# Two orders of work on TensorE, in both layers of a two-layer model: projections around the router product, and transposes ahead of the intra products

## The chip, the core and the metric

The kernel runs on one core of a Trainium2 chip. The metric is the device time of one execution in microseconds. Its engines are TensorE (matrix products and transposes, with its weight loads), VectorE, ScalarE, GpSimd, and SyncE, which here only issues transfers. Each runs its own list of instructions in order and waits on semaphores that the others raise.

## The reference, cut to what matters

Two layers over 2 sequences of 2048 tokens of 256 numbers. Each layer normalizes its input and adds two branches to it.

```
x = L0_attn_x;  xn = layernorm(x)
x = x + mamba_block(xn) + soft_tree(xn)          # layer 0
xn = layernorm(x)
x = x + mamba2(xn) + expert_choice_moe(xn)       # layer 1

# layer 0's first branch
h = rmsnorm(xn);  v = xn + mamba2(h)             # 8 heads of 64, state 16, conv of 3 taps
mamba_block = v + silu(rmsnorm(v) @ mlp_w1 + b1) @ mlp_w2 + b2

# mamba2, for both layers
z, xBC, dt = split(h @ W_in);  dt = softplus(dt + dt_bias)
x, B, C = split(silu(causal_conv(xBC)))
state_t = state_{t-1} * exp(dt_t * A) + dt_t * x_t (outer) B_t
y_t = state_t . C_t + D * x_t
return rmsnorm(y * silu(z)) @ W_out              # layer 1: 4 heads of 128, state 64, 4 taps

# soft_tree: gate = sigmoid(xn @ Wq @ routers.T) over 255 nodes, leaf probabilities as
# products along 8 levels, @ leaf_values @ Wout
# moe: softmax(xn @ Wr), each of 8 experts takes its 1024 best tokens, gelu MLP, scatter-add
```

## The kernel before, in words

**Layer 0** goes over the tokens in 8 steps of 512, each of four chunks (tiles) of 128 tokens. A step has a front (mamba2 and the gates of the tree, for step f) and a back (tree output, MLP, next norm and router, for step b = f - 1). Both are in one loop body, written out by hand for each engine: `step0(f, b, n)` for TensorE stands at L2224, for ScalarE at L1113, for VectorE at L1614, where its arguments are (n, f, b). n = f + 1 is the step whose start is done at the end of the body. Steps 2 to 6 run in a hardware loop, the others are written out.

The order on TensorE around the change, at the end of a body: down products of the MLP; turned rows of n (hT); dt product of n; `in_proj(n, 0)`, which gives the B and C columns; the transposes of the next-layer rows (nT); the router product on nT (L2295). Then, in the next body, where n has become f: `decay_log_sums` (L2110: three products of 32 columns and one transpose, which wait for VectorE's softplus chain), `in_proj(f, 1)` to `in_proj(f, 4)` (the four blocks x0 to x3 of x), the transposes of the MLP's normed input (`turned(b, "h2T", ...)`), the gate products, and four of the eight up-products of the MLP (`up`, L2196). An up-product needs h2T in a high and a low half: ScalarE copies the high half h2Th (L1126), VectorE subtracts it for the low half h2Tl (L1629).

PSUM is used in four banks for these: two for the front, two for the back, each pair in turns. `open_front` and `open_back` let TensorE write a bank only when its last content has been read (for a projection: by both copies that ScalarE makes in `raw`, L1026; for an up-product: by the SiLU in ScalarE's `up`, L1107).

ScalarE's order at the same place: for n, turned rows, the exponential for dt, `raw(n, 0)`; the two nT copies; the exponential of the router's softmax; then in the next body `decay_exp`, `raw` of 1 to 4, the two h2T copies, the SiLUs of the convolutions and the tanh of the gates, and the SiLUs of the up-products among them. VectorE's order, which the diff leaves alone: dt and softplus, the copies of the router product and the softmax, the scores; then `normed` (xo, L1622), convolutions 0 to 3, `h2T_low`, convolution 4, the scans and chunks.

**Layer 1** (its mamba2) goes over 32 tiles of 128 tokens, four in a step, 8 steps, all written out (L2408 to L2433). For tile n TensorE does: `chunk1(n + 1)` (z, the turned x block xt, the small products, in steps 0 to 4 also a count product for the search of the experts' thresholds); `recur1(n)` (the product with the state, "inter"; the new state; the intra products E times Xdt); `y_turned1(n - 1)`, transposes of the gated y; in the first two tiles of a step two projections of the next step; `project1(n - 1)`, which waits for ScalarE's copy yT of the turned rows. In the third tile of a step the fifth projection comes ahead of `chunk1`. xt of tile n + 2 shares a bank with the state product of tile n, which VectorE reads in its state update (L1937). VectorE's sum of y (L1927) waits for the intra products; GpSimd then gates y (L938), makes the rms factor of the tile before (L946), and VectorE mixes (L1948).

The experts of layer 1 come last, from about 1183 us on; the change does not touch them.

Of the kernel before, what the change touches and what calls it, by code (L numbers as in the profile page):

```python
# [143 lines left out]
def program(nc, d, out):  # L144
    ctx = ExitStack()
    with ctx:
# [867 lines left out]
        def _(act):  # L1014
# [98 lines left out]
            def step0(f, b, n):  # L1113
# [14 lines left out]
                if f is not None:  # L1128
                    decay_exp(L, s, f)
                    for j in range(1, 5):  # L1130
                        raw(L, s, f, j)
                if b is not None:
                    h2T_copies()
                if f is not None:
                    conv_silu(L, s, f, 0)
                    conv_silu(L, s, f, 1)
                    gates(L, s, f)
                for j in EARLY_UPS:
                    if f is not None and j < 3:
                        conv_silu(L, s, f, j + 2)  # L1140
                    if b is not None:
                        up(b, j)
# [23 lines left out]
                if b is not None:  # L1166
                    for k in range(2):
                        p = back_wait(act, b, f"nT{k}")

                        back_wait(act, b - 1, "rt1")  # L1170
                        nT_stored.wait_ge(act, b, 0)
                        a.activation(nT[:, :, 2 * P * k:2 * P * (k + 1)],
                                     p[:, :].rearrange("p (k n) -> p k n", k=KD), ACT.Copy).then_inc(nT_sig.sem, 1)
                    smx_sig.wait_ge(act, b, 1)
                    a.activation(sx[:, 1, :, :], sx[:, 0, :, :], ACT.Exp).then_inc(sme_sig.sem, 1)
# [3 lines left out]
            raw(LAYERS[0], sets[0], 0, 0)  # L1179
            step0(0, None, 1)  # L1180
# [891 lines left out]
        def _(pe):  # L2072
# [151 lines left out]
            def step0(f, b, n):  # L2224
                L, s = LAYERS[0], sets[0]

                if f is not None:
                    decay_log_sums(L, s, f)
                    for j in range(1, 5):
                        in_proj(L, s, f, j)  # L2230
                if b is not None:
                    turned(b, "h2T", xo, h2_sig, CH)
                if f is not None:
                    gates(L, s, f)
# [41 lines left out]
                if b is not None:  # L2276
                    for g in range(2):
# [6 lines left out]
                        back_filled(last, f"nT{g}")  # L2284
                    for g in range(2):
# [10 lines left out]
            in_proj(LAYERS[0], sets[0], 0, 0)  # L2296
            step0(0, None, 1)
# [57 lines left out]
            def recur1(i, c):  # L2355
                q, cb, n = c % 2, CB[i % 2], CH * i + c
# [6 lines left out]
                filled1(mm(p[0:64, :], Bs[:, q, :], Xs[:, q, :]), "state")  # L2363
# [44 lines left out]
            for n in range(TILES1):  # L2408
# [7 lines left out]
                if n:  # L2416
                    y_turned1(*divmod(n - 1, CH))
                if following and c < 2:
# [145 lines left out]
```

## Time and profile before

| | us |
|---|---|
| median of 3 runs | 1607.27 |
| runs | 1602.73, 1607.27, 1607.95 |
| the profiled execution | 1599.53 |
| its span, from first to last instruction | 1597.7 |

The profile is of the one execution in the third line. Its page gives the busy time of each engine as a share of the span. In this kernel layer 0 fills about the first 785 us, the mamba part of layer 1 runs to about 1183 us, the experts to the end. PE is TensorE's matrix unit and PEld its weight loads, DVE is VectorE, ACT is ScalarE, POOL is GpSimd, SPq is SyncE's queue. A row of a timeline gives the start, the duration, the engine, the source line and the operation with its output and inputs, how many instructions it merges, and in brackets the idle time just before it with the instruction that ended it. Many products share the helper's line L2076; they are told apart by their operands: `hT,m0wbc` is projection 0 of layer 0, `hT,m0big` with 16 instructions are the projections x0 to x3 (two weight blocks, each in two instructions), `wr,nT` the router product, `h2Th,w1h` the first of an up-product's six, `EW,hT` the gates.

### The profile page before, as it was taken

Reading aid. Unit: us, or ns where it says so; the run is one execution under the profiler, and the core shown is the slowest. Engines: PE = TensorE matmul, PEld = TensorE weight load, DVE = VectorE, ACT = ScalarE, POOL = GpSimd, SP = SyncE. Lnnn points to the kernel's source line nnn. Section 1 sums busy time; section 2 is a strip of 40 time slices with the busy share of each in tenths; the row PEclk is TensorE's granted clock in tenths of the full one; section 3 lists DMA queues with packets and bytes.
Section 4 is the critical chain, followed back from the end, with each engine's and each line's share of the span. In section 5 each row is a group of like instructions: output and inputs, shape, how many; then the busy total and the mean of one; then the engine's idle time right before and its main releaser. Section 6 shows DMA issues by size and latency. Waiting matters only on the chain.

```text
span 1597.7 us, 22669 instructions
## 1 busy us (share of the span) xinstructions
PE 1462.5 (92%) x7315; PEld 1062.9 (67%) x7315; DVE 1082.6 (68%) x2557; ACT 725.6 (45%) x1468; POOL 534.0 (33%) x631
## 2 busy tenths in 40 slices
PE   4879999999999999997788888999889999999996
PEld 2546767677676867676544555555459888898895
DVE  4878677686867676762588888878865555546542
ACT  1434252524334252522165556555455555555552
POOL 1242424142433424231112233233343434544343
PEclk8999999999999999997799999999999999999998
DMA  6110030302021120201221111212023334343332
GB/s 212 53 54 27 20 100 1 106 13 93 26 82 37 39 80 0 94 14 40 95 93 37 66 63 37 66 63 67 27 62 99 61 87 106 77 97 62 87 54 27
DMA packets 71846, 100.90 MB, mean 63 GB/s; under 512 B 13000, under 2 KB 58192, under 8 KB 71760
## 3 DMA queue, kind: packets, MB, share of 16 engines
q1 hardware_dynamic: 59472, 82.77, 15.9%
q0 software_dynamic: 12288, 17.05, 6.4%
q8 instruction: 46, 0.75, 0.2%
q14 instruction: 40, 0.33, 0.1%
HBM read 74.30 MB, written 25.49 MB: 62 GB/s over the span
## 4 chain that ended last, share of the span: by engine, by line
PE 63%; issue 15%; DVE 8%; POOL 7%; ACT 4%; DMA 1%; SPq 1%; PEldq 0%; POOLq 0%; ACTq 0%; DVEq 0%; PEld 0%
PE bank L2076 59%; POOL yb L938 2%; POOL Xs L930 2%; POOL ry L946 1%; PE bank L2186 1%; PE bank L2443 1%; PE bank L2154 1%; DVE am L1890 1%; POOL out L994 1%; DVE dts L1497 1%; PE bank L2212 1%; ACT am L1111 1%; ACT tg L1072 1%; POOL ry L943 1%; ACT u L1049 0%
## 5 line engine op out<-in xcount | busy, mean ns | idle before, releaser
L2031 DVE TENSOR_TENSOR aml<-m0big,amh 128x512 fp32r<-128x512 f32 x128 | 88.2, 689 | 162.8 <-ACT amh L1327 153.3
L994 POOL DMA_INDIRECT out<-EW,IDX x64 | 105.1, 1643 | 223.7 <-DVE EW L2016 209.0
L1322 ACT ACTIVATE m0big<-bank,eb 128x512 f32<-128x512 f32 x128 | 88.0, 687 | 147.6 <-PE bank L2076 125.6
L2076 PE MATMUL bank<-w2h,amh 128*128 128x256 f32 x512 | 147.9, 289 | 0.0
L2076 PE MATMUL bank<-w2h,aml 128*128 128x256 f32 x512 | 144.8, 283 | 0.0
L2076 PE MATMUL bank<-w2l,amh 128*128 128x256 f32 x512 | 144.7, 283 | 0.0
L2076 PE MATMUL bank<-EW,am 128*128 128x256 f32 x512 | 115.8, 379 | 0.0
L1111 ACT ACTIVATE am<-bank,b 128x512 f32<-128x512 f32 x64 | 43.7, 683 | 150.0 <-PE bank L2076 149.4
L2076 PEld LDWEIGHTS bank<-EW,am 128*128 128x128 f32 x512 | 97.2, 190 | 13.5 <-ACT am L1111 0.3
L2076 PE MATMUL bank<-xTh,w1h 128*128 128x512 f32 x256 | 102.3, 399 | 2.8 <-DVE w1l L2022 2.8
L2076 PEld LDWEIGHTS bank<-w2h,amh 128*128 128x128 f32 x512 | 97.6, 191 | 8.3 <-issue 5.8
L2076 PE MATMUL bank<-xTl,w1h 128*128 128x512 f32 x256 | 100.6, 393 | 0.0
L2076 PE MATMUL bank<-xTh,w1l 128*128 128x512 f32 x256 | 99.6, 389 | 0.0
L2076 PEld LDWEIGHTS bank<-w2l,amh 128*128 128x128 f32 x512 | 97.8, 191 | 2.2
L938 POOL TENSOR_TENSOR yb<-yb,zs 128x512 f32<-128x512 f32 x32 | 40.6, 1269 | 171.8 <-DVE yb L1927 171.8
L2076 PEld LDWEIGHTS bank<-w2h,aml 128*128 128x128 f32 x512 | 97.7, 191 | 0.0
L2076 PEld LDWEIGHTS bank<-Xdt,E 128*128 128x128 f32 x512 | 64.3, 201 | 42.9 <-issue 38.9
L1327 ACT ACTIVATE amh<-m0big 128x512 fp32r<-128x512 f32 x128 | 80.9, 632 | 4.0
L2076 PE MATMUL bank<-Xs,Bs 128*64 128x512 f32 x128 | 72.3, 648 | 11.3 <-POOL Xs L930 6.6
L834 POOL TENSOR_TENSOR xb<-x,xp 128x256 f32<-128x256 f32 x32 | 22.4, 728 | 172.3 <-ACT u L1049 164.3
L2076 PE MATMUL bank<-EW,yT 128*128 128x256 f32 x256 | 62.5, 387 | 13.1 <-ACT yT L1248 12.4
L969 POOL DMA_INDIRECT xg<-rows_d,IDX x64 | 67.1, 1048 | 19.3 <-issue 19.0
(336 smaller groups left out, 3695.9 us busy)
## 6 DMA issues: line engine op xcount, KB each, us to landing
EW<-in_e_w SPq DMA_DIRECT2D x16, 1024.0 KB, 5.9
dA0b<-dA_d SPq DMA_DIRECT2D x16, 512.0 KB, 3.8
E<-dA_d SPq DMA_DIRECT2D x16, 512.0 KB, 5.4
m0big<-dA_d SPq DMA_DIRECT2D x16, 512.0 KB, 4.7
xin<-in_L_attn_x SPq DMA_DIRECT2D x8, 512.0 KB
xp<-in_L_attn_x SPq DMA_DIRECT2D x8, 512.0 KB, 3.9
rows_d<-xo SPq DMA_DIRECT2D x8, 512.0 KB, 3.0
x_d<-xb SPq DMA_DIRECT2D x8, 512.0 KB, 4.1
```

The costliest lines, as they stand in the source:

```text
L834: g.tensor_tensor(xb[:, c, :], x2[:, c, :], xp[:, c, :], ALU.add).then_inc(xb_sig.sem, 1)
L930: g.tensor_tensor(Xs[:, q, :].rearrange("p (h e) -> p h e", h=NH1), x3, WEND[:, hd].unsqueeze(2).to_broadcast([P, NH1, P]), ALU.mult).then ...
L938: g.tensor_tensor(yb[:, q, :], yb[:, q, :], zs[:, q, :], ALU.mult).then_inc(s1.yg.sem, 1)
L943: g.tensor_scalar(ry[:, c:c + 1], ssq[:, c:c + 1], 1.0 / DI, 1e-5, ALU.mult, ALU.add).then_inc(s1.rv.sem, 1)
L946: g.tensor_tensor(ry[:, c:c + 1], ry[:, c:c + 1], nhalf[:, 0:1], ALU.pow).then_inc(s1.ry.sem, 1)
L969: g.indirect_dma_start(out=xg[:, q, c, :], out_offset=None, in_=rows_d, in_offset=bass.IndirectOffsetOnAxis(ap=IDX[:, 4 * u + c:4 * u + c ...
L994: g.indirect_dma_start(out=out_rows, out_offset=bass.IndirectOffsetOnAxis(ap=IDX[:, 4 * u + c:4 * u + c + 1], axis=0), in_=ye[:, q, c, :], ...
L1111: a.activation(am[:, k, :], p[:, :], ACT.Silu, bias=b1[:, k:k + 1]).then_inc(am_sig.sem, 1)
L1322: a.activation(am2[:, j % 2, :], bank[j % 2][:, :], ACT.Gelu, bias=eb1[:, u // 2, j:j + 1]).then_inc(gelu_sig.sem, 1)
L1327: a.activation(amh[:, j % 4, :], am2[:, j % 2, :], ACT.Copy).then_inc(am_high.sem, 1)
L2031: v.tensor_tensor(aml[:, j % 4, :], am2[:, j % 2, :], amh[:, j % 4, :], ALU.subtract).then_inc(am_low.sem, 1)
L2076: return t.matmul(out_, lhsT, rhs, start=first, stop=last)
```

## The change

In layer 0 the projection x0 of the next step moves from the start of the next body to the end of this one, between the nT transposes and the router product. The start of a body becomes: x1, decay sums, x2, h2T transposes, x3, gates. ScalarE's copies move in the same way: `raw(n, 1)` behind the nT copies and ahead of the router's exponential; then `raw` 2, `decay_exp`, `raw` 3, h2T copies, `raw` 4. Each of ScalarE's early up-SiLUs goes ahead of the convolution's SiLU that stood before it. For the first step, x0 is done ahead of the first body. In layer 1 `recur1` is cut in two, and the transposes `y_turned1(n - 1)` go between the state product and the intra products.

```diff
@@ ScalarE, step0
                 if f is not None:
+                    raw(L, s, f, 2)
                     decay_exp(L, s, f)
-                    for j in range(1, 5):
-                        raw(L, s, f, j)
+                    raw(L, s, f, 3)
                 if b is not None:
                     h2T_copies()
                 if f is not None:
+                    raw(L, s, f, 4)
                     conv_silu(L, s, f, 0)
                     conv_silu(L, s, f, 1)
                     gates(L, s, f)
                 for j in EARLY_UPS:
+                    if b is not None:
+                        up(b, j)
                     if f is not None and j < 3:
                         conv_silu(L, s, f, j + 2)
-                    if b is not None:
-                        up(b, j)
...
+                if n is not None:
+                    raw(L, s, n, 1)
+                if b is not None:
                     smx_sig.wait_ge(act, b, 1)
                     a.activation(sx[:, 1, :, :], sx[:, 0, :, :], ACT.Exp).then_inc(sme_sig.sem, 1)
...
             raw(LAYERS[0], sets[0], 0, 0)
+            raw(LAYERS[0], sets[0], 0, 1)
             step0(0, None, 1)
@@ TensorE, step0
                 if f is not None:
+                    in_proj(L, s, f, 2)
                     decay_log_sums(L, s, f)
-                    for j in range(1, 5):
-                        in_proj(L, s, f, j)
+                    in_proj(L, s, f, 3)
                 if b is not None:
                     turned(b, "h2T", xo, h2_sig, CH)
                 if f is not None:
+                    in_proj(L, s, f, 4)
                     gates(L, s, f)
...
                         back_filled(last, f"nT{g}")
+                if n is not None:
+                    in_proj(L, s, n, 1)
+                if b is not None:
                     for g in range(2):
                         p = open_back(pe, b, f"rt{g}")
...
             in_proj(LAYERS[0], sets[0], 0, 0)
+            in_proj(LAYERS[0], sets[0], 0, 1)
             step0(0, None, 1)
@@ TensorE, layer 1
                 p = open1("state", n)
-                filled1(mm(p[0:64, :], Bs[:, q, :], Xs[:, q, :]), "state")
+                filled1(mm(p[0:64, :], Bs[:, c % 2, :], Xs[:, c % 2, :]), "state")
+
+            def intra1(i, c):
+                q = c % 2
                 s1.y0.wait_ge(pe, i, c)
                 s1.xdt.wait_ge(pe, i, c + 1)
                 s1.M.wait_ge(pe, i, c + 1)
...
                 recur1(i, c)
                 if n:
                     y_turned1(*divmod(n - 1, CH))
+                intra1(i, c)
```

## Rows read from the trace of the kernel before

**Rows 1.** The page: busy time and share of each engine; one DMA issue.

```profile
PE 1462.5 (92%) x7315; PEld 1062.9 (67%) x7315; DVE 1082.6 (68%) x2557; ACT 725.6 (45%) x1468; POOL 534.0 (33%) x631
...
dA0b<-dA_d SPq DMA_DIRECT2D x16, 512.0 KB, 3.8
```

**Rows 2.** Timeline of TensorE, boundary into step 4: start, duration, instruction, idle before.

```profile
373.53 1.96 PE L2076 MATMUL bank<-hT,m0wbc 128*128 128x512 f32 x4
375.33 1.04 PE L2282 MATMUL bank<-ident,xo 128*128 128x128 f32 x8
377.43 1.93 PE L2076 MATMUL bank<-wr,nT 128*128 128x12 f32 x16 [1.06 <-ACT nT L1172]
...
380.35 8.73 PE L2076 MATMUL bank<-hT,m0big 128*128 128x512 f32 x16
...
389.79 3.62 PE L2076 MATMUL bank<-EW,hT 128*128 128x256 f32 x16
393.06 0.58 PE L2076 MATMUL bank<-h2Th,w1h 128*128 128x512 f32 x1
...
397.05 0.50 PE L2076 MATMUL bank<-h2Th,w1h 128*128 128x512 f32 x1 [0.86 <-ACT am L1111]
```

**Rows 3.** Windows: busy time of PE, PEld, DVE, ACT, POOL; PEclk; DMA share; GB/s.

```profile
382.00:384.00 2.00, 2.00 (x3) 0.78 (x3) 1.97 (x6) 0.27 (x1) 0.00 (x0) 0.50 0.64 55
...
1000.00:1002.00 2.00, 2.00 (x7) 1.29 (x7) 1.96 (x6) 0.34 (x2) 0.00 (x0) 0.54 0.95 356
```

**Rows 4.** Timeline of ScalarE, the same boundary.

```profile
376.68 1.08 ACT L1172 ACTIVATE nT<-bank 128x512 f32<-128x512 f32 x2
...
390.27 1.08 ACT L1126 ACTIVATE h2Th<-bank 128x512 fp32r<-128x512 f32 x2
```

**Rows 5.** Timeline of VectorE, the same boundary and the first chunk behind it.

```profile
379.33 0.27 DVE L1708 COPY rtb<-bank 128x24 f32<-128x24 f32 x2
...
382.86 1.53 DVE L1461 SCALAR_TENSOR_TENSOR u<-xbuf,m0conv,u 128x512 f32<-128x512 f32 x2
...
385.03 1.54 DVE L1461 SCALAR_TENSOR_TENSOR u<-xbuf,m0conv,u 128x512 f32<-128x512 f32 x2 [0.25 <-ACT xbuf L1039]
...
390.90 1.29 DVE L1629 TENSOR_TENSOR h2Tl<-bank,h2Th 128x512 fp32r<-128x512 f32 x2 [0.40 <-ACT h2Th L1126]
...
404.24 0.17 DVE L1555 COPY Bs<-bank 128x16 f32<-128x16 f32 x1 [7.60 <-PE bank L2162]
```

**Rows 6.** Timeline of SyncE's queue, the same boundary: the first load of decay rows.

```profile
386.05 0.34 SPq L665 DMA_DIRECT2D dA0b<-dA_d  x1
```

**Rows 7.** Timeline of TensorE at the boundaries into steps 0, 1 and 2.

```profile
53.67 1.98 PE L2076 MATMUL bank<-m0big,hT 128*128 128x512 f32 x4 [1.73 <-ACT tg L1072]
...
108.73 0.64 PE L2076 MATMUL bank<-dtv,triU 128*128 128x32 f32 x2 [5.01 <-DVE dtv L1509]
...
126.40 0.47 PE L2076 MATMUL bank<-h2Th,w1h 128*128 128x512 f32 x1 [2.75 <-DVE h2Tl L1629]
...
198.42 2.38 PE L2076 MATMUL bank<-wr,nT 128*128 128x12 f32 x16 [1.06 <-ACT nT L1172]
...
219.32 0.50 PE L2076 MATMUL bank<-h2Th,w1h 128*128 128x512 f32 x1 [0.86 <-ACT am L1111]
```

**Rows 8.** Timeline of VectorE at the boundary into step 1.

```profile
115.18 1.54 DVE L1461 SCALAR_TENSOR_TENSOR u<-xbuf,m0conv,u 128x512 f32<-128x512 f32 x2 [3.75 <-ACT xbuf L1039]
```

**Rows 9.** Waits of TensorE, 780 to 1200 us: total us, times, longest us.

```profile
PE bank L2076 <- ACT yT L1248: 12.4, 18, 0.7
```

**Rows 10.** Timeline of TensorE in layer 1, step 3, behind a third and a fourth tile.

```profile
996.32 0.63 PE L2345 MATMUL bank<-ident,u 128*128 128x128 f32 x4 [2.51 <-DVE S L1937]
...
1003.52 1.99 PE L2076 MATMUL bank<-EW,yT 128*128 128x256 f32 x8 [0.69 <-ACT yT L1248]
```

**Rows 11.** Timeline of VectorE in layer 1: in step 3, and in step 6's first tile.

```profile
1008.29 0.16 DVE L1805 TENSOR_SCALAR okm<-bank 128x3 int32<-128x3 f32 x1 [0.76 <-PE bank L2353]
...
1105.33 3.12 DVE L1890 SCALAR_TENSOR_TENSOR am<-xbuf,m1conv,am 128x512 f32<-128x512 f32 x4 [1.67 <-ACT xbuf L1204]
```

More of the change, by code:

```diff
@@ L2355, in recur1 @@
             def recur1(i, c):
-                q, cb, n = c % 2, CB[i % 2], CH * i + c
+                cb, n = CB[i % 2], CH * i + c
                 s1.bs.wait_ge(pe, i, c + 1)
```

## The prediction

> **What bounds the kernel now.** I read the busy shares first: TensorE is the busiest engine by far [rows 1]. A busy TensorE is modelled, though, so the next view is its own order of work over one boundary between two steps of layer 0, with its idle time. There it stands idle 1.06 us for the next-layer rows nT, ahead of the router product, and 0.86 us ahead of the third up-product, until ScalarE has emptied the bank of the first [rows 2]. The same two waits stand in the boundary into step 2 and in the ones after it, six in all, within 0.1 us [rows 7]. Third, the granted clock: behind the short products (router, decay sums) TensorE drops to 1.2 GHz, level 0.50, for over 3 us [rows 3]. Its 16 projection instructions there take 8.73 us; by the four of the first projection, (1.96 - 0.24) / 4 = 0.43 each with a tail of 0.24, they would take 7.1, so this costs 1.6 us [rows 2]. From there to the next boundary TensorE has no wait over 0.4 us: layer 0 is TensorE-bound except in those places.
>
> In layer 1, TensorE's list of waits has 18 of 0.69 us for yT [rows 9]; between them it waits for VectorE's state update, 2.51 us in the place shown, one of six [rows 10]. There the two engines take turns as the bound.
>
> **Layer 0, a steady boundary** (the times are those of the boundary into step 4). The eight nT transposes end near 376.2 (0.9 us from 375.33). Today TensorE then waits until 377.43 [rows 2]. With projection x0 there (four instructions, 1.7 us) it reaches the router product at 377.9, when ScalarE's nT copies (376.68 to 377.76) are done [rows 4]. So the 1.06 wait is filled, and the router product comes 0.5 us later, ending at 379.8. Projection x1 covers the wait for the decays; then the sums (0.8), x2 (1.7), the h2T transposes (0.9), x3 (1.7), the gates (3.3): TensorE could start the up-products at about 390.0, against 393.06 now [rows 2]. Here I assume full clock: full-width projections now stand among the short products.
>
> But the up-products wait for the low half of h2T, which VectorE makes behind the normed rows and four convolutions, and the change leaves VectorE's order alone. Today it is done at 390.90 + 1.29 = 392.2 [rows 5], hidden under the gates. In the changed order the router's copy on VectorE, at 379.33 today, gets its second half only at about 379.8, so softmax, score rows and normed rows come 0.35 us later. The convolutions lose their waits, 0.25 before the second and 0.40 before h2Tl [rows 5], because x0 and x1 are ready early and h2Th, which ScalarE copies at 390.27 today [rows 4], is ready before 387. That makes 392.2 + 0.35 - 0.65 = 391.9, and the up-products start at 392.0 instead of 393.06: **1.05 us won**, with a new TensorE wait of 2 us in front of them. The clock's 1.6 us hide in that wait, so whether the low stretch goes changes little.
>
> The up-products themselves: ScalarE today does the last projection's copies, two h2Th copies, a table load, five SiLUs and four tanhs without rest, and so reads the first up-bank late. The third product starts at 397.05; six instructions at the pace of the others (0.23 each, twice) after 393.06, with 0.2 for the first, would let it start at 396.02. That is **1.03 us to win**: with h2Th copied before the last projection, and each up-bank read ahead of a convolution's SiLU, ScalarE is through with the tanhs at 392.6 and reads the first bank at 393.8, before the third product is due at 394.9. Bounds: 0.6 if ScalarE stays half behind, 1.2 if the start is smoother.
>
> Together 2.1 us. The lower bound is 1.0 (the ScalarE part alone), the upper 3.7 (1.06 + 1.6 + 1.03, all of TensorE's, were VectorE no limit). I take 2.1, by VectorE's own rows. Five such boundaries give 10.5. The boundary into step 2 has a longer low stretch: from the router product to the third up-product it takes 219.32 - 198.42 = 20.90 us against 19.62 later [rows 2, 7], so 1.3 more may go there: 3.4.
>
> What the moved work drags along: the decays' exponentials come 2.2 us later on ScalarE, behind x1's copies. On SyncE the first load of them is issued at 386.05 today [rows 6]; 2.2 later and with 3.8 to land [rows 1] they are there at 392.1. VectorE's first scan wants them at 393.5, and has 7.60 us of idle time behind it [rows 5]. The next-layer stores stand ahead of this on SyncE's queue and wait for nothing that comes later but the score rows, by 0.35. GpSimd's residual sum waits for the last SiLU, which comes earlier. All free; if that cover were gone, each us past it would count.
>
> **Layer 0, the first boundaries.** Into step 1, TensorE waits 5.01 us for the decays, then 2.75 for h2Tl, behind VectorE's preparation of weights [rows 7]. With x0 and x1 in the first wait, VectorE loses its 3.75 us wait before the second convolution [rows 8]. But TensorE then idles some 7 us before the up-products and starts them at 1.2 GHz, which takes 1.7 to 3.4 us back. I take 1.5. Into step 0 two projections come ahead of the sums; later TensorE stalls 1.73 us for the tanhs [rows 7], and this is what can be won: 1.7, between 0 and 2.5. **Layer 0: 10.5 + 3.4 + 1.5 + 1.7 = 17.1 us.**
>
> **Layer 1.** In the third and fourth tile of each step, and in all of the last, the order is intra products (1.0 us), y transposes (0.44), a copy on ScalarE (0.60), project, which waits 0.69 [rows 9, 10]. With the transposes first, the intra products cover the copy and project starts 0.85 earlier. What that is worth:
> - third tiles: TensorE then waits for VectorE's state anyway (2.51, [rows 10]). Nothing.
> - fourth tiles of steps 0 to 4: VectorE waits 0.76 us for TensorE's count product behind them [rows 11], so 0.76 each: 3.8.
> - step 5: both gains pass into VectorE's wait of 1.67 us for a projection [rows 11]: 1.5.
> - steps 6 and 7: VectorE and GpSimd mostly set the pace with the one-hot rows: 1.6, between 0 and 3.
> - The intra products end 0.44 later. VectorE asks for them later still in nearly all tiles. Free; 0.44 a tile (32 tiles: 14 us) if I misread this.
>
> Sum 6.9. Against it stands the clock: behind the 2.51 us wait TensorE fell to 1.2 GHz (granted 0.54 from 1000 to 1002) [rows 3]. That wait grows to 3.4, and I charge one further low stretch like that of layer 0: 1.7. **Layer 1: 5.2 us**, between -1 and 9.
>
> The Trainium skill, "TensorE: Matmul & The Clock Gate", Part 1 (The HAM clock gate) and the section on HAM oscillation, has TensorE throttled by default, released by activity, and cold again behind an idle gap; that speaks against both new waits. The trace agrees in layer 1, while in layer 0 the clock fell behind short products and a wait of only 1.06 us. [...]
>
> **The sum:** 17.1 + 5.2 = 22.3, say 22 us. The profiled execution took 1599.5 us (span 1597.7 and 1.8 around it); it would become 1577.5. It lies 8 us under the median of the runs shown, 1607.3, and below all three; on the median the forecast is 1607.3 - 22 = **1585 us**.
>
> **The rivals.**
> - *The router's delay eats VectorE's lead* (0.17): the copy chain behind the later router product costs as much as the saved waits. A boundary gives 1.0, layer 0 gives 5.0 + 2.3 + 3.2 = 10.5, in all 16: 1591. For it: that chain has hardly a gap. Against: the 0.65 us of waits are plain rows.
> - *TensorE alone sets layer 0* (0.08): no new wait before the up-products; 5 x 3.7 + 5.0 + 3.2 + 5.2 = 32: 1575. Against it: the four convolutions in a row.
> - *Layer 1 gives nothing* (0.12), all absorbed by VectorE: 1590.
> - *The change doesn't do what it says* (0.05): h2T is turned early but VectorE reaches it no sooner and ScalarE stays behind, and layer 1's transposes wait for GpSimd's gated rows in their new place. Some 3 us: 1604.
> - *Slower, by the clock* (0.05): the new 2 us wait puts the up-products at 1.2 GHz, and layer 1's longer waits do the same. Price: two low stretches a boundary, at the 1.7 each, are 6 x 3.4 = 20, and two more in each of five steps of layer 1 are 17; 37 against the 24 (17.1 + 6.9) won: 1620. It decides from 48 us of new low time, half of it lost. For it: layer 1's rows. Against: the wait stands between gates and up-products, both dense.
>
> **How the numbers follow.** The forecast has 0.53. The range from 1570 (a little under the second rival) to 1600 leaves out the last two rivals and the edges of the others, under 2 in 10. A measurement of this kernel can tell 0.3%, 4.8 us, from no change. Faster by more: the forecast and the first three rivals, less a little at their edge, 0.88. Within it: the fourth and that edge, 0.07. Slower: 0.05.
>
> **What the profile of the changed kernel would show.** At each steady boundary: no wait before the router product; a wait of 1 to 2 us for h2Tl before the first up-product; none for am before the third; steps 86.8 us apart instead of 88.9. In layer 1: the 0.69 us waits gone, the waits for the state some 0.8 longer. The prediction is wrong if the steps come 85 or 88 us apart, if the wait before the up-products carries another name than h2Tl, or if the granted clock is 0.50 inside the up-products.

## The result, and the profile after

| | before | after |
|---|---|---|
| median, us | 1607.0 | 1578.5 |
| runs, lowest to highest, us | 1602.7 to 1608.0 | 1576.5 to 1581.2 |
| the profiled execution, us | 1599.5 | 1576.5 |
| its span, us | 1597.7 | 1574.6 |

The ratio of after to before is 0.984, 95% interval 0.982 to 0.986: faster by 25.7 us of 1607, between 22.5 and 28.9. The forecast was 1585, 22 us. To see where the 23 us of the two profiled executions lie, I cut both traces at three places: the first product of each projection 0 in layer 0, the first of layer 1, and the first of the experts.

| stretch, us | before | after | won | forecast |
|---|---|---|---|---|
| to projection 0 of step 1 | 101.8 | 99.4 | 2.4 | 1.7 |
| to that of step 2 | 92.8 | 90.5 | 2.3 | 1.5 |
| to that of step 3 (boundary into step 2) | 90.15 | 85.7 | 4.45 | 3.4 |
| one steady step, to that of step 4, 5, 6 and 7 (four of them) | 88.9 | 86.3 | 2.6 | 2.1 |
| from projection 0 of step 7 to layer 1 | 148.5 | 144.0 | 4.5 | 2.1 |
| layer 0 | 788.6 | 764.7 | 23.9 | 17.1 |
| layer 1, mamba part | 398.4 | 398.3 | 0.1 | 5.2 |
| experts | 410.7 | 411.6 | -0.9 | 0 |

The page of after, busy time of each engine, against [rows 1]:

```profile
PE 1453.0 (92%) x7315; PEld 1061.9 (67%) x7315; DVE 1079.9 (69%) x2557; ACT 727.3 (46%) x1468; POOL 533.4 (34%) x631
```

TensorE does the same 7315 products in 9.5 us less busy time. By stretch, it is 15.9 us less in layer 0 (717.0 to 701.1), where the granted clock rose from 0.95 to 0.97, and 5.4 more in layer 1's mamba part, where it fell from 0.96 to 0.93. How much of the 9.5 us is the clock's wasn't taken apart. Its timeline at the boundary into step 4 answers to [rows 2]:

```profile
361.91 1.96 PE L2081 MATMUL bank<-hT,m0wbc 128*128 128x512 f32 x4
363.71 1.04 PE L2288 MATMUL bank<-ident,xo 128*128 128x128 f32 x8
364.58 1.88 PE L2081 MATMUL bank<-hT,m0big 128*128 128x512 f32 x4
366.31 1.85 PE L2081 MATMUL bank<-wr,nT 128*128 128x12 f32 x16
...
374.82 3.62 PE L2081 MATMUL bank<-EW,hT 128*128 128x256 f32 x16
380.05 0.50 PE L2081 MATMUL bank<-h2Th,w1h 128*128 128x512 f32 x1 [1.61 <-DVE h2Tl L1634]
...
386.66 0.66 PE L2217 MATMUL bank<-ident,leaf 128*128 128x128 f32 x4 [0.34 <-ACT am L1111]
```

The wait ahead of the router product is gone, and so is the one ahead of the third up-product; a wait of 1.61 us for h2Tl stands before the first. VectorE at the same place, against [rows 5]:

```profile
370.56 1.14 DVE L1627 TENSOR_SCALAR xo<-x,ry 128x256 f32<-128x256 f32 x4 [0.51 <-issue]
371.62 1.53 DVE L1466 SCALAR_TENSOR_TENSOR u<-xbuf,m0conv,u 128x512 f32<-128x512 f32 x2
...
376.86 1.53 DVE L1466 SCALAR_TENSOR_TENSOR u<-xbuf,m0conv,u 128x512 f32<-128x512 f32 x2
378.43 0.23 DVE L1477 TENSOR_SCALAR xbuf<-xbuf,flags 128x2 f32<-128x2 f32 x1
378.63 1.29 DVE L1634 TENSOR_TENSOR h2Tl<-bank,h2Th 128x512 fp32r<-128x512 f32 x2
```

Four convolutions in a row, then h2Tl without a wait: from 371.62 to h2Tl VectorE has no gap over 0.2 us. In layer 1, TensorE behind a third tile (step 3) and behind the next, against [rows 10], and the clock of the first of these stretches:

```profile
971.68 1.09 PE L2355 MATMUL bank<-ident,u 128*128 128x128 f32 x4 [3.44 <-DVE S L1942]
...
977.46 1.02 PE L2388 MATMUL bank<-ident,yb 128*128 128x128 f32 x4
978.31 1.05 PE L2081 MATMUL bank<-Xdt,E 128*128 128x128 f32 x8
979.20 1.95 PE L2081 MATMUL bank<-EW,yT 128*128 128x256 f32 x8
980.99 1.88 PE L2081 MATMUL bank<-EW,hT 128*128 128x512 f32 x4
982.71 0.60 PE L2355 MATMUL bank<-ident,u 128*128 128x128 f32 x4
```

```profile
971.60:975.00 3.40, 3.32 (x11) 2.39 (x11) 1.49 (x6) 2.23 (x6) 2.03 (x4) 0.50 0.18 48
975.00:978.40 3.40, 3.40 (x8) 1.23 (x8) 3.26 (x10) 1.75 (x6) 0.00 (x0) 0.52 0.82 295
978.40:981.80 3.40, 3.40 (x19) 2.77 (x18) 2.50 (x7) 0.60 (x1) 1.27 (x1) 1.00 0.01 4
```

The products of the transposed y start with no wait. But the wait for the state is 3.44 us instead of 2.51, and TensorE runs at 1.2 GHz (granted 0.50 and 0.52) for twice as long behind it, 6.8 us against 3.4. From the end of the wait to the next tile it needs 982.71 - 971.68 = 11.03 us; before it was 1007.07 - 996.32 = 10.75.

### The profile page after: what moved, and what is told of

Its sections match the earlier page's. It is cut to its first block, busy times and chain, and to the rows that moved or that the text cites. A ratio compares the mean times of both kernels' runs of the same rounds, so it can differ in the third digit from the quotient of the medians.

```text
span 1574.6 us, 22674 instructions
## 1 busy us (share of the span) xinstructions
PE 1453.0 (92%) x7315; PEld 1061.9 (67%) x7315; DVE 1079.9 (69%) x2557; ACT 727.3 (46%) x1468; POOL 533.4 (34%) x631
## 4 chain that ended last, share of the span: by engine, by line
PE 63%; issue 15%; DVE 10%; POOL 7%; ACT 2%; DMA 1%; SPq 0%; DVEq 0%; PEldq 0%; POOLq 0%; PEld 0%; ACTq 0%
PE bank L2081 59%; DVE u L1466 3%; POOL yb L938 2%; POOL Xs L930 2%; POOL ry L946 1%; PE bank L2191 1%; PE bank L2457 1%; PE bank L2159 1%; DVE am L1895 1%; POOL out L994 1%; DVE xo L1627 1%; PE bank L2288 1%; POOL ry L943 1%; PE bank L2135 0%; SPq L586 0%
## 5 line engine op out<-in xcount | busy, mean ns | idle before, releaser
L2081 PE MATMUL bank<-Xdt,E 128*128 128x64 f32 (+1 forms) x512 | 69.0, 285 | 0.0
```

The lines of the kernel that those rows point to most:

```text
L2081: return t.matmul(out_, lhsT, rhs, start=first, stop=last)
```

## The experiments

Each run is given with its ratio to the kernel before, 95% interval behind it, and the landmarks of its profiled execution ("layer 0" is the time at which layer 1's first projection starts, "layer 1" from there to the experts). "Step" is the distance of projections 0 in the steady part of layer 0. A "low stretch" is a time in which TensorE's granted clock is 0.50 (1.2 GHz).

**Each layer alone.** Layer 1 back in the old order:

```diff
-            def intra1(i, c):
-                q = c % 2
                 s1.y0.wait_ge(pe, i, c)
...
-                intra1(i, c)
```

> The changed kernel without its layer 1 part. In the changed kernel's trace layer 0 ends 23.9 us earlier than before (first product of layer 1 at 764.7 instead of 788.6), and the mamba part of layer 1 takes 398.3 instead of 398.4 us. Theory: all of the gain is layer 0's, so this kernel is as fast as the changed one: 23 to 28 us faster than before, ratio 0.984 +- 0.002, with layer 1 at 398 us and single low stretches of the clock. Rival (layer 1 wins 5 us when alone, and layer 0's new timing spoils it by chance of phase): this one loses 5 us against the changed kernel, ratio 0.988.

Measured: 0.9858 (0.9832 to 0.9884), 1584.9 us. Step 86.3, layer 0 770.5, layer 1 402.1, with low stretches of 10.2 us in two places instead of the single ones expected. The other half, layer 1's edit on the kernel before:

> The kernel before with the y transposes ahead of the intra products, alone. Theory: the 0.69 us waits for yT go, the wait for VectorE's state grows to 3.4 us and the stretch at 1.2 GHz behind it doubles, so that nothing is left: 0 to 1 us, ratio 1.000, layer 1 at 398 us. Forecast of the prediction: 5.2 us, ratio 0.997. If the low stretches stay single here, 4 us faster.

Measured: 0.9983 (0.9965 to 1.0001), 1601.1 us. Step 88.85, layer 0 788.8, layer 1 398.6, with low stretches of 6.8 us behind the waits for the state, as the theory had it.

So layer 0 carries 22.8 us (1.42% of 1606; 18.6 to 27) and layer 1 alone 2.7 us, hardly to be told from nothing. That the profiled executions give 18.1 and 23.9 us for the same code of layer 0 (with and without layer 1's edit) was a surprise that has its own paragraph below.

**Layer 0 taken apart.** First x0 of the next step ahead of the router product, with the last projection (x3) and each early up-SiLU left where they were, and layer 1 in the old order (the cut shows ScalarE, against the kernel after):

```diff
+                    raw(L, s, f, 4)
                 if b is not None:
                     h2T_copies()
                 if f is not None:
-                    raw(L, s, f, 4)
...
-                    if b is not None:
-                        up(b, j)
                     if f is not None and j < 3:
                         conv_silu(L, s, f, j + 2)
+                    if b is not None:
+                        up(b, j)
```

and in_proj(f, 4) ahead of the h2T transposes on TensorE.

> The kernel before with projection x0 of the next step ahead of the router product and x1 ahead of the decay sums, alone: h2T is turned behind all projections, and ScalarE's up-SiLUs keep their old places. Theory by the trace (what counts is x0 early: it fills the 1.06 us wait, feeds VectorE's convolutions and ScalarE's copies): the up-products start 1.4 us earlier, and the wait of the third up-product shrinks from 0.86 to 0.3 or less, as ScalarE ends its h2T copies 3 us earlier; steps 86.4 to 86.9 us apart against 88.9, 18 to 22 us in all, ratio 0.987. Rival (the turning of h2T is needed for the ScalarE part, 1.0 to 1.2 per boundary): steps 87.5 apart, 10 to 13 us, ratio 0.993.

Measured: 0.9846 (0.9818 to 0.9873), 1582.5 us. Step 86.26, layer 0 769.0: a little more than the theory had, and far from the rival's 87.5. Its boundary into step 4:

```profile
377.68 3.62 PE L2081 MATMUL bank<-EW,hT 128*128 128x256 f32 x16
382.92 0.50 PE L2081 MATMUL bank<-h2Th,w1h 128*128 128x512 f32 x1 [1.62 <-DVE h2Tl L1634]
```

From its projection 0 (364.78) to this first up-product it is 18.14 us, and in the kernel after 380.05 - 361.91 = 18.14 too. Then the other part by itself, h2T turned ahead of the last projection and up-SiLUs first, with x0 at its old place:

> The kernel before with h2T turned ahead of the last projection and ScalarE's early up-SiLUs ahead of the convolutions' SiLUs, alone; x0 stays behind the decay sums. Theory: the 1.06 us wait and the low clock stay, the up-products start where they did (the gates end there), and only the 0.86 us wait for am goes: steps 87.8 apart, 1.0 to 1.2 per boundary, 7 to 8 us in all, ratio 0.995. Rival (turning h2T early is the main part, since VectorE waited 0.40 us for it): 1.5 or more per boundary, 11 us, ratio 0.993.

Measured: 0.9951 (0.9932 to 0.997), 1597.5 us. Step 88.25 (87.8 expected), but 86.55 in one, that from 284.28 to 370.83. The boundary at the start of that step, and the next one, with the clock of each:

```profile
288.17 1.93 PE L2077 MATMUL bank<-wr,nT 128*128 128x12 f32 x16 [1.06 <-ACT nT L1173]
...
291.09 5.32 PE L2077 MATMUL bank<-hT,m0big 128*128 128x512 f32 x12
...
305.47 0.50 PE L2077 MATMUL bank<-h2Th,w1h 128*128 128x512 f32 x1 [0.24 <-ACT am L1111]
...
374.73 1.93 PE L2077 MATMUL bank<-wr,nT 128*128 128x12 f32 x16 [1.06 <-ACT nT L1173]
...
377.78 6.87 PE L2077 MATMUL bank<-hT,m0big 128*128 128x512 f32 x12
...
393.71 0.50 PE L2077 MATMUL bank<-h2Th,w1h 128*128 128x512 f32 x1 [0.24 <-ACT am L1111]
```

```profile
292.00:294.00 2.00, 2.00 (x6) 0.90 (x5) 1.44 (x6) 0.99 (x2) 0.00 (x0) 1.00 0.40 17
...
378.00:380.00 2.00, 2.00 (x3) 0.79 (x3) 1.29 (x7) 0.40 (x2) 0.00 (x0) 0.50 0.14 10
```

Both boundaries have the same waits; the one has its 12 projection instructions in 5.32 us, the other in 6.87. That is a clean price for a low stretch of 3.4 us on TensorE's path: 88.25 - 86.55 = 1.70 us. The reorder itself gives 88.86 - 88.25 = 0.6 a step, not the 1.0 to 1.2 expected, since the third up-product's wait shrinks from 0.86 to 0.24. On top of x0's move it gives nothing: both kernels have steps of 86.3.

To see whether the filled wait of 1.06 us was what counted, x0 of the next step also moved to the end of the body, but behind the router product, so that the wait stays:

```diff
-                if n is not None:
-                    in_proj(L, s, n, 1)
                 if b is not None:
                     for g in range(2):
                         p = open_back(pe, b, f"rt{g}")
...
+                if n is not None:
+                    in_proj(L, s, n, 1)
```

(ScalarE's `raw(n, 1)` likewise behind the router's exponential; the rest as in the run with x0 alone.)

> Layer 0 only: projection x0 of the next step at the end of the body, but behind the router product instead of ahead of it (and ScalarE's copies of it behind the router's exponential); the rest as in the run with x0 alone, whose steps are 86.3 us apart. The 1.06 us wait for nT comes back, and the router's copy on VectorE is no longer delayed by 0.38 us. Theory (VectorE's chain sets the boundary, so TensorE's wait is worth nothing by itself; feeding the convolutions early is what counts): steps 85.9 to 86.3 apart, if the clock stays up. Rival (filling the 1.06 us wait is the gain): steps 87.2 to 87.4 apart. If the clock falls here again for 3.4 us, up to 0.5 us on top in either case, as the wait for h2Tl hides most of it.

Measured: 0.9952 (0.9934 to 0.997), 1598.3 us. Step 88.51, and 86.77 in the one step (283.07 to 369.84) without a low stretch. A step with one, and the clock there:

```profile
373.74 1.99 PE L2080 MATMUL bank<-wr,nT 128*128 128x12 f32 x16 [1.06 <-ACT nT L1173]
...
392.99 0.50 PE L2080 MATMUL bank<-h2Th,w1h 128*128 128x512 f32 x1 [0.85 <-ACT am L1111]
```

```profile
377.00:379.00 2.00, 2.00 (x3) 0.67 (x2) 1.30 (x7) 0.00 (x0) 0.00 (x0) 0.53 0.14 10
```

This boundary has no wait for h2Tl: with the 1.06 us wait and the low stretch in place TensorE is itself late enough. It costs 88.51 - 86.26 = 2.25 us a step against x0 ahead of the router product, and 1.74 of it goes when the clock stays up. The other 0.51 is neither the theory's (85.9 to 86.3 at full clock) nor the rival's (87.2 to 87.4). The step without a low stretch shows where it lies:

```profile
283.07 1.96 PE L2080 MATMUL bank<-hT,m0wbc 128*128 128x512 f32 x4
...
286.97 1.93 PE L2080 MATMUL bank<-wr,nT 128*128 128x12 f32 x16 [1.06 <-ACT nT L1173]
...
300.87 0.49 PE L2080 MATMUL bank<-h2Th,w1h 128*128 128x512 f32 x1
...
304.52 0.50 PE L2080 MATMUL bank<-h2Th,w1h 128*128 128x512 f32 x1 [0.60 <-ACT am L1111]
```

From projection 0 to the first up-product it is 300.87 - 283.07 = 17.80 us here, although the wait for nT is still there; in the kernel after, without that wait, it is 18.14. The run with h2T turned early and x0 at its old place has 17.82 in its step without a low stretch (302.10 - 284.28). So at the first up-product the wait costs nothing by itself as long as VectorE is the limit; what it costs comes with the low stretch (19.16 us with one). The 0.51 lies behind it: from the first up-product to the second group of turned leaves it is 7.45 us here and 6.61 in the kernel after, 0.84 more, with a wait of 0.60 us for ScalarE ahead of the third up-product. Whether the low stretch goes because the wait is filled, or because a projection now stands between the transposes and the router product, no run separates. With the wait in place the low stretch was absent in one or two of the six boundaries of these two runs; with x0 ahead of the router product it was absent in all of them.

**VectorE as the new bound of the boundary.** On the kernel after, h2Tl is made one convolution earlier:

```diff
-                    for j in range(4):
+                    for j in range(3):
                         conv(L, s, f, j, dve0)
                         keep_halo(L, s, f, j)
...
                     h2T_low()
-                    conv(L, s, f, 4, dve0)
-                    keep_halo(L, s, f, 4)
+                    for j in range(3, 5):
+                        conv(L, s, f, j, dve0)
+                        keep_halo(L, s, f, j)
```

> The changed kernel with one move on VectorE: the low half of h2T (h2Tl) ahead of the fourth convolution instead of behind it. Theory: in the changed kernel VectorE's chain sets when the up-products start, TensorE waiting 1.6 us for h2Tl at each steady boundary; h2Th is there 2.2 us before VectorE takes it. So this wait goes: steps 84.7 us apart instead of 86.3, about 10 us in all, ratio 0.978 against before. Rival (TensorE's own products, or ScalarE's SiLUs behind the later fourth convolution, take over at once): steps 85.8 or more, under 3 us.

Measured: 0.9771 (0.9745 to 0.9797), 1567.2 us: 37 us under before by the ratio, and 11 under after. Step 84.90, layer 0 755.4. VectorE, and TensorE's up-products, at the same boundary:

```profile
370.57 1.53 DVE L1466 SCALAR_TENSOR_TENSOR u<-xbuf,m0conv,u 128x512 f32<-128x512 f32 x2
372.34 1.29 DVE L1634 TENSOR_TENSOR h2Tl<-bank,h2Th 128x512 fp32r<-128x512 f32 x2
```

```profile
370.23 3.62 PE L2082 MATMUL bank<-EW,hT 128*128 128x256 f32 x16
...
376.87 0.50 PE L2082 MATMUL bank<-h2Th,w1h 128*128 128x512 f32 x1
```

No row between those two of TensorE carries a wait. 88.86 - 84.90 = 3.96 us a boundary: this is what TensorE's own waits and low stretch were worth, the 3.7 of the prediction's second rival. The first up-product comes 373.76 - 357.33 = 16.43 us behind projection 0, where it was 19.53 before and 18.14 after: with VectorE out of the way the filled wait counts too.

**Layer 1: what took the gain.** To keep TensorE's clock up, the z product of a step's first tile (which waits for the state of the third tile before) is preceded by two repeats of itself; the real product overwrites them.

```diff
                 p = open1("z", n)
+                if c == 0 and i:
+                    for _ in range(2):
+                        for k in range(KD):
+                            mm(p[:, :], (hT, h2T)[i % 2][:, k, cols(c)], W[1]["z"][:, k, :], k == 0, k == 1)
```

On the kernel after:

> The changed kernel with filler work in layer 1: ahead of the first tile of each step but step 0, TensorE does the z products twice more (8 instructions, 3.4 us, same bank, their result written over), where it now waits 1.7 to 4.1 us for VectorE's state. Nothing else changes. Theory (the gain of the moved transposes in layer 1 is eaten by the clock, which falls to 1.2 GHz for 6.8 us behind this wait): the low stretches there go, and the mamba part of layer 1 takes 393 us instead of 398.3, 1.0 us less in each of six steps, until VectorE sets the pace. Rival (VectorE absorbs it, the clock costs nothing): 397.5 us or more.

Measured: 0.9833 (0.9808 to 0.9859), 1577.3 us. Layer 1 395.75, between the two readings. TensorE's waits for the state between 780 and 1180 us there, and in the kernel after without the repeats (total us, times, longest):

```profile
PE bank L2359 <- DVE S L1942: 5.5, 7, 0.9
```

```profile
PE bank L2355 <- DVE S L1942: 19.5, 7, 4.1
```

On the kernel before:

> The kernel before with the same filler in layer 1. Its waits there are 0.7 to 3.2 us, so up to 2.7 us of the filler stand on the path in step 5 and 1 us in the others. Theory (clock): the low stretches, 3.4 us each, go; layer 1 takes 394 to 397 instead of 398.4, and 1 to 3 us more than the changed kernel with filler, because each 0.69 us wait for yT in the fourth tiles is still there. Rival (VectorE sets the pace once the clock is held, whatever the order of the transposes): the same 393 as the changed kernel with filler.

Measured: 0.9981 (0.9964 to 0.9998), 1603.9 us. Layer 1 398.45, with no low stretch behind 819 us: over the 394 to 397 of the theory. The totals say little by themselves; the steps of layer 1 say more (us between projections 0, in brackets the length of the low stretch in it):

| step of layer 1 | before | after | before, repeats | after, repeats |
|---|---|---|---|---|
| 0 | 48.2 (6.8) | 47.1 (6.8) | 45.7 | 45.6 |
| 1 | 48.1 (3.4) | 48.2 (6.8) | 47.5 | 48.3 (3.4) |
| 2 | 47.9 (3.4) | 48.1 (6.8) | 47.5 | 48.2 (3.4) |
| 3 | 47.9 (3.4) | 48.1 (6.8) | 47.5 | 46.7 |
| 4 | 44.7 | 46.4 (6.8) | 47.2 | 45.2 |
| 5 | 45.5 | 44.1 | 48.9 | 46.9 |

In the new order the low stretches cost 1.2 to 1.5 us a step where the repeats removed them (steps 0, 3 and 4). In steps 1 and 2 one of 3.4 us is left, and nothing is won; in step 5, which had none, the repeats cost 2.9 us. In the old order the repeats won 2.4 us in step 0 and 0.4 to 0.6 in each of steps 1 to 3, so its low stretches cost something too. But in steps 4 and 5, where it waited 0.7 us or not at all, they stand on TensorE's path and cost 2.5 and 3.4. So 398.32 - 395.75 = 2.6 us and 398.45 - 395.75 = 2.7 us are sums of gains and losses. What the new order would be worth at full clock throughout, and so whether the 6.9 us that I had summed were right, these two runs leave open. The waits in the kernel before, in the same view:

```profile
PE bank L2345 <- DVE S L1937: 13.6, 6, 3.2
PE bank L2076 <- ACT yT L1248: 11.7, 17, 0.7
```

Of the 17 waits for yT one is left in the kernel after, 11.0 us less; the waits for the state took 19.5 - 13.6 = 5.9 of this back, and the lower clock about the rest. The windows over all of layer 1's mamba part have a granted clock of 0.96 before and 0.93 after:

```profile
788.60:1187.00 398.40, 350.26 (x1362) 200.41 (x1362) 336.43 (x816) 221.83 (x556) 119.22 (x136) 0.96 0.18 59
```

```profile
764.70:1163.00 398.30, 355.63 (x1362) 204.96 (x1362) 336.19 (x815) 223.96 (x556) 117.03 (x136) 0.93 0.18 60
```

The same 1362 products were 5.4 us longer busy.

**Making the state earlier.** The wait for the state is long in the third tile because VectorE does the fifth convolution of the next step ahead of it. On the kernel with h2Tl earlier:

```diff
-                if following and c == 2:
-                    conv1(i + 1, 4)
                 sums1(i, c)
+                if following and c == 2:
+                    conv1(i + 1, 4)
```

> The kernel with h2Tl ahead of convolution 3, and besides, in layer 1's third tile, VectorE makes the sum of y and the state before the fifth convolution of the next step instead of behind it. Theory 1 (the state wait is VectorE's order: the convolution, about 3.1 us, stands in front of the state): the state comes 3.1 us earlier, TensorE's waits of 3.4 us behind the third tiles fall under 0.5, the convolution fills VectorE's 1.31 us wait for GpSimd's rms factor, and layer 1 goes from 398.5 to 386 to 392 us. Theory 2 (VectorE's total of work sets layer 1 and its waits only move): under 3 us, the waits for the state turn up in the fourth tile instead, layer 1 at 396 to 399.

Measured: 0.9833 (0.98 to 0.9866), 1576.3 us. Layer 1 405.65: 7 us longer, a miss of both theories. TensorE, ScalarE and VectorE in the place where the wait for the state was:

```profile
965.81 1.11 PE L2356 MATMUL bank<-ident,u 128*128 128x128 f32 x4 [4.02 <-ACT u L1219]
```

```profile
965.13 0.63 ACT L1219 ACTIVATE u<-u 128x512 f32<-128x512 f32 x1 [6.07 <-DVE u L1896]
```

```profile
962.59 2.51 DVE L1896 SCALAR_TENSOR_TENSOR u<-xbuf,m1conv,u 128x512 f32<-128x512 f32 x3
...
968.01 0.16 DVE L1811 TENSOR_SCALAR okm<-bank 128x3 int32<-128x3 f32 x1 [2.22 <-PE bank L2364]
```

TensorE needs both results of VectorE there, the state and, through ScalarE's SiLU u, the fifth convolution. The two take VectorE 5.3 us in either order, so whichever comes second ends at the same time, and the convolution has the SiLU of 0.63 us behind it: the wait went from 3.44 to 4.02 us. Step 0 and steps 2 to 4 are 0.4 to 0.7 us longer, about this growth. The rest of the 7 us lies in step 1 (50.1 against 48.2 us, with a low stretch of 10.2 us instead of 6.8) and in step 5 (46.6 against 44.1, with a new wait of 1.48 us for u and a low stretch of 3.4 behind it). The convolution does fill VectorE's wait for GpSimd, but the wait for TensorE behind it (okm) grew from 0.53 to 2.22. The bracket of a wait names the last releaser alone; the one behind it was some 2 us away. The same edit with layer 1 in the old order, and h2Tl earlier with layer 1 in the old order:

> Both: the state ahead of the fifth convolution, layer 1's transposes in the old order. If the new order was worth nothing only because the state's wait behind it took its gain back, then with the state early it is worth 2 to 7 us: this one is that much slower in layer 1 than the one with the new order. If it is worth nothing for another reason, both take the same within 1.5 us.

> The kernel with h2Tl ahead of convolution 3, with layer 1 in the old order (y's transposes behind the intra products). If the new order of layer 1 is worth nothing while the state comes late, this takes the same time within 2 us, layer 1 398 to 400. If it has a worth that only the clock hides (2.7 us by the runs with the clock held up), layer 1 is 0 to 3 us longer than with it.

Measured: 0.9829 (0.9789 to 0.9869), 1574.8 us, layer 1 406.8; and 0.9787 (0.9756 to 0.9817), 1572.9 us, layer 1 401.5. The first is 1.1 us longer in layer 1 than its pair with the new order, which is its second reading (no worth for another reason than the late state), and by ratio there is nothing between them (0.9829 and 0.9833). The second is 3.0 longer. Of those, 2.8 lie ahead of step 0 (34.3 us from the first projection 0 to the next, against 31.6), where this execution has a low stretch of 17.1 us and its pair one of 6.8, and 1.0 in step 0 (48.1 against 47.1); later steps give 0.8 back. Steps 1 to 3 take 47.9 to 48.2 us in both. By ratios, h2Tl earlier with and without the new order differ by 0.0016, 2.6 us, within the intervals.

**The best two together.** h2Tl earlier, and the repeats in layer 1:

> The kernel with h2Tl ahead of convolution 3, and in layer 1 two extra repeats of the z product (their result is overwritten by the real one) ahead of the wait for the state in the first tile of each step, so that TensorE doesn't stand idle there. If layer 1's clock costs the new order 2.6 us and nothing of that depends on layer 0: layer 0 at 755.4 us as without the filler, layer 1 at 395.8 instead of 398.5, and a profiled execution of 1562 to 1563.5. If the extra products cost as much as the clock gives back: layer 1 at 398 to 399. Layer 0 is to be the same in either case.

Measured: 0.9771 (0.9749 to 0.9792), 1569.9 us. Layer 1 396.1 as expected; but the profiled execution took 1569.6 us, not 1562 to 1563.5, since layer 0 ended at 759.8 instead of 755.4, with the same steps of 84.90 and a first step that ended 3.1 us later. The kernel with h2Tl earlier alone is as fast, and simpler.

**What the first step does from run to run.** After and the kernel with its layer 0 alone run the same instructions up to layer 1. Their clock, in windows of 5 us from 60 us on (after, then the other):

```profile
65.00:70.00 5.00, 5.00 (x17) 2.29 (x17) 5.00 (x8) 2.18 (x5) 0.70 (x2) 0.81 0.00 0
70.00:75.00 5.00, 5.00 (x28) 3.79 (x27) 4.96 (x8) 0.00 (x0) 2.41 (x3) 1.00 0.00 0
```

```profile
65.00:70.00 5.00, 5.00 (x15) 2.92 (x14) 4.89 (x9) 2.08 (x5) 0.57 (x2) 0.50 0.00 0
70.00:75.00 5.00, 5.00 (x11) 1.89 (x11) 2.53 (x5) 0.32 (x1) 2.17 (x3) 0.50 0.00 0
75.00:80.00 5.00, 5.00 (x19) 4.46 (x19) 1.88 (x3) 0.00 (x0) 0.00 (x0) 0.54 0.00 0
```

Behind the same wait of 2.30 us TensorE ran at 1.2 GHz for 3.4 us in the one execution and for 17 in the other, and projection 0 of step 1 started at 99.4 and at 105.0. Layer 0 then ended at 764.7 and 770.5, 5.8 us apart: nearly all of it from this one place.

## Why the prediction was right, and where its sizes were off

**The steady boundary** (2.1 forecast, 2.6 measured). The mechanism stands as written: the 1.06 wait filled, no low stretch, and VectorE's h2Tl as the new limit with a wait of 1.61 (2 forecast). The normed rows came 0.38 us later against projection 0 (370.56 - 361.91 = 8.65, before 381.80 - 373.53 = 8.27; forecast 0.35). The term that was too small is VectorE's: I took 0.65 for its lost waits, and from the first convolution to h2Tl it took 378.63 - 371.62 = 7.01 us against 390.90 - 382.86 = 8.04, 1.03 less. Beside the two waits with a bracket, small gaps ahead of the second and third convolution, which carry none, went as well; the start times of [rows 5] would have shown them. So the up-products start 1.39 earlier, not 1.05. What brought TensorE to VectorE's limit is less clear than I wrote. The sum has the filled wait do it, with the clock hidden behind it. But in the two runs in which the wait stayed and the clock happened to stay up, the first up-product came just as early (17.80 and 17.82 us behind projection 0, against 18.14), so the clock alone is enough. Whether the filled wait alone would be, no run shows.

**The third up-product** (1.03 forecast). From the first up-product to the second group of turned leaves it is 386.66 - 380.05 = 6.61 us, before 7.81: 1.20 won, the upper bound that I gave. But the reason was wrong in part. I put it down to the moved SiLUs and the earlier h2Th copies; the run with x0 alone has neither move, and a step of 86.26 us (its h2Th copies still come 3.4 us earlier against projection 0, since the projections do). What does it is mainly TensorE's wait of 1.6 us, in which ScalarE catches up: the run with x0 behind the router product has x0's copies off this stretch too, but not that wait, and its third up-product still waits 0.85 us. The part of the change that turns h2T earlier brings nothing here as long as VectorE is the limit.

**The rival "TensorE alone sets layer 0"** did not happen, for the reason given against it, and its size of 3.7 us was right: 3.96 when h2Tl comes one convolution earlier.

**Into step 2 and the rest of layer 0.** 4.45 won against 3.4: the longer low stretch went whole. Into steps 0 and 1 4.7 went against 3.2 in these two executions. The first part (2.4) can't be called shown, since the start of step 1 moves by up to 5.6 us between executions of the same code. The second (2.3) holds in its sign: the step behind it took 92.3 to 94.0 us in three executions with the old layer 0 and 90.5 and 90.8 in two with the new one. Its details were off: TensorE waited 1.90 us for the decays and then 3.05 for h2Tl, not some 7. Behind the last projection 0 I had counted one steady boundary, and 4.5 went: some 2 more, where the low stretch behind the last boundary lasted 13.7 us instead of 17.1. That part is luck of the execution: the kernel before with layer 1's edit, which has the old layer 0, had 13.7 there too and took 147.1 us instead of 148.5.

**Layer 1** (5.2 forecast; 0.1 between the profiled executions, 2.6 to 2.9 by three pairs of ratios, each within its own interval). The term of the sum that failed is the clock's: I charged one further low stretch, 1.7 us in all. The longer wait for the state doubled the low stretch in steps 1 to 3 (6.8 us for 3.4) and put one of 6.8 into step 4, which had none. In steps 1 to 3 the whole of the gain went there (48.1 us a step in both kernels), step 4 got 1.7 us longer, and only steps 0 and 5 won (1.05 and 1.4). The term "fourth tiles of steps 0 to 4, 0.76 each" came out in step 0 alone, where VectorE's wait for the count product fell from 2.10 to 0.89 us; in steps 2 and 3 it is 0.82 and 0.67 still, against 0.85 and 0.76. The prediction had the growth of the wait right (3.4) and had this very mechanism as its last rival; the price belonged in each of the four steps, not once.

Why the ratios show more than the two profiles: of six profiled executions with the old order of layer 1 and no other edit of it, four had one or two low stretches of 10.2 or 17.1 us where the others have 3.4 or 6.8, and took 401.5 to 402.1 us; the kernel before was one of the two without (398.4 and 398.6). The three with the new order had none and took 398.3 to 398.6. That the new order keeps these long stretches away is not shown by three executions.

**The rule on idle gaps.** The Trainium skill, "TensorE: Matmul & The Clock Gate", Part 1 (The HAM clock gate), has a TensorE cold again behind an idle gap, if it is long enough; the prediction held it against both new waits. In layer 1 the trace agrees (1.2 GHz for 6.8 us behind 3.44 us of waiting). In layer 0 the length of the gap doesn't sort the cases: the new wait of 1.61 us before the up-products left the clock at full speed in every steady boundary, while a wait of 1.06 us ahead of the router product was followed by a low stretch, though not in every boundary of the same kernel. What stands around the wait differs: gates and up-products in the one place, transposes and short products in the other. That this decides is argued from the order of work; the runs show only the places.

**The sum.** Layer 0 took 22.8 us by the timed run of it alone (17.1 forecast), layer 1 2.7 (5.2): 25.5 against 22.3, and 25.7 measured for both. Two errors of opposite sign made the total look better than its parts. The median of after lies 6.5 us below the forecast, within the range: 3.7 from the gain, and most of the rest because the two medians are 28.5 us apart where the ratio gives 25.7.

## What to carry to other kernels

When an edit moves the bound to another engine, read that engine's list next: here one convolution put behind h2Tl was worth 11 us more, on top of the 26 of the change, for a swap of two calls. Before putting work ahead of a wait that exists anyway, price the longer wait in the clock too, for each place where it stands. And the name in the bracket of a wait is the last releaser, not the only one: when the state was made earlier at the cost of the fifth convolution, that convolution became the one that TensorE waits for, and layer 1 got 7 us longer.

## What the runs showed of the hardware that I had not expected

- The length of a low stretch behind one and the same wait is not fixed. Behind a 2.30 us wait in the first step it was 3.4 us in one execution and 17 in another of the same instructions; in layer 1's old order it was 3.4 us in most steps and 10.2 in one step of some executions, which made that step 50.8 us instead of 48.0. Two profiled executions with the same layer 0 thus differ by 5.8 us at its end, before the kernels differ at all, more than several of the edits here are worth.
- A low stretch of 3.4 us costs 1.70 to 1.74 us where TensorE is the bound (88.25 - 86.55, 88.51 - 86.77), and less where VectorE shares the bound: a step of layer 1 in the old order took 47.9 to 48.1 us with one and 47.5 with repeated products in its place, a part of which may itself stand on the path.
- Idle time may cost less when it is filled with products that nobody reads (2.6 us in layer 1 of the new order), and more where there was little idle time to fill (2.5 and 3.4 us in two steps of the old one). In the timed ratios the first is 0.9833 against 0.984, not to be told apart.
